# The softmax loop of a hybrid transformer block: one errand in each slot, behind the context products

## What is computed

```python
x = jnp.transpose(query, (1, 0, 2)).reshape(sq * b, h)     # sq = 512, b = 4, h = 256
mixed = (x @ Wqkv.T).reshape(sq, b, nh, 3, hn)             # nh = 16 heads of hn = 16
q, k, v = mixed[..., 0, :], mixed[..., 1, :], mixed[..., 2, :]
# each to (b * nh, sq, hn)
attn = jax.nn.softmax(jnp.einsum('gqd,gkd->gqk', q, k) * norm, axis=-1)
ctx = jnp.einsum('gqk,gkd->gqd', attn, v)
out = ctx.reshape(...) @ Wproj.T + bproj
```

## Time and profile before

| | us |
|---|---|
| time, median of 3 runs | 1167.54 (1164.84 to 1168.75) |
| profiled execution, its own time | 1167.14 |
| its span in the profile | 1165.3 |
| softmax loop, from slot 0 of group 1 to slot 5 of group 7 | 188.6 |
| PE, DVE, ACT busy in the span | 1126.4, 939.7, 774.3 |
| waits of transposed scores (PE's weight loads) for exponentials in the loop | 34.5 |

### The profile page before, as it was taken

The page is one execution under the profiler, slowest core; times in us unless marked ns, Lnnn a source line. Parts: engine busy times, 40 slices in busy tenths (PEclk is TensorE's granted clock), DMA queues, the critical chain, the costliest instruction groups (busy, mean ns, idle before and its releaser), DMA issues. The chain is left out here.

```text
span 1165.3 us, 22548 instructions
## 1 busy us (share of the span) xinstructions
PE 1126.4 (97%) x7599; PEld 908.6 (78%) x7599; DVE 939.7 (81%) x2141; ACT 774.3 (66%) x1535; POOL 629.9 (54%) x1070
## 2 busy tenths in 40 slices
PE   8999999998988999999999999999999999999898
PEld 7444444346766899999999999999999999999876
DVE  6888887866568888888888888888888888888862
ACT  3467676773447767776777777676777677676633
POOL 4020500001715776877786786777687777767520
PEclk9999999999999999999999999999999999999999
DMA  6333333301220102112110201110211211011120
GB/s 186 56 56 57 56 56 57 56 2 38 80 70 23 48 33 84 33 49 69 45 36 33 84 33 49 69 48 33 84 33 43 74 33 48 33 48 33 33 72 1
DMA packets 23450, 60.51 MB, mean 52 GB/s; under 512 B 3367, under 2 KB 8359, under 8 KB 22183
## 3 DMA queue, kind: packets, MB, share of 16 engines
q1 hardware_dynamic: 23335, 59.07, 18.8%
HBM read 44.67 MB, written 2.33 MB: 40 GB/s over the span
## 5 line engine op out<-in xcount | busy, mean ns | idle before, releaser
L1823 DVE SCALAR_TENSOR_TENSOR ln_xn<-l_proj_q,par,ln_xn 128x511 f32<-128x511 f32 (+2 forms) x192 | 142.9, 744 | 97.9 <-ACT ln_xn L1707 95.5
L778 DVE TENSOR_REDUCE a_neg_max<-a_scores 128x1 f32<-128x512 f32 x244 | 155.0, 684 | 30.8 <-PE a_scores L433 28.9
L678 ACT ACTIVATE a_probs<-a_scores_t 128x512 f32<-128x512 f32 x256 | 138.5, 599 | 58.5 <-PE a_scores_t L455 57.3
L96 POOL TENSOR_SCALAR ln_var_eps<-ln_mean_var 128x4 f32<-128x4 f32 (+1 forms) x13 | 3.0, 230 | 283.2 <-DVE ln_mean_var L86 193.3
L1713 ACT ACTIVATE ln_xn<-ln_xn,par 128x512 f32<-128x512 f32 x128 | 92.6, 724 | 94.9 <-DVE ln_xn L1823 94.9
L1412 POOL TENSOR_TENSOR l_k_tok<-l_normed,k_norm 128x384 f32<-128x384 f32 x63 | 64.0, 1016 | 153.9 <-ACT l_normed L1724 153.9
L1823 DVE SCALAR_TENSOR_TENSOR ln_xn<-l_proj_k,par,ln_xn 128x511 f32<-128x511 f32 (+2 forms) x192 | 143.5, 747 | 4.5
L1724 ACT ACTIVATE l_normed<-l_turn_q,l_shift,l_scale 128x128 f32<-128x128 f32 x252 | 95.0, 458 | 21.6 <-POOL l_shift L1405 21.5
L1403 POOL TENSOR_TENSOR l_scale<-l_small,l_minus_half 128x8 f32<-128x8 f32 x64 | 105.1, 1642 | 5.0
L1724 ACT ACTIVATE l_normed<-l_turn_k,l_shift,l_scale 128x128 f32<-128x128 f32 x252 | 95.9, 482 | 0.0
L1781 ACT ACTIVATE l_gate<-l_proj_gv 128x512 f32<-128x512 f32 x64 | 38.2, 597 | 79.0 <-PE l_proj_gv L1491 79.0
(11 more groups left out here) (401 smaller groups left out, 3536.6 us busy)
## 6 DMA issues: line engine op xcount, KB each, us to landing
l_keep<-keep_rows SPq DMA_DIRECT2D x64, 448.0 KB, 3.5
a_stack<-a_dense SPq DMA_DIRECT2D x90, 128.0 KB, 4.3
head_raw<-w_heads SPq DMA_DIRECT2D x8, 1024.0 KB, 6.7
x_tok<-x SPq DMA_DIRECT2D x4, 512.0 KB, 8.2
wo_raw<-w_o SPq DMA_DIRECT2D x1, 2048.0 KB, 10.8
out<-x_tok SPq DMA_DIRECT2D x1, 1920.0 KB
a_stack<-a_max_rows_t SPq DMA_DIRECT2D x64, 4.0 KB
ctx_tok<-w_qkv SPq DMA_DIRECT2D x1, 768.0 KB, 6.7
```

The source lines that it names most:

```text
L678: act.activation(probs[:, n % 2, h, :], scores_t[(4 * n + h) % TURNS][:], ACT.Exp, scale=SOFT_SCALE).then_inc(probs_done, 1)
L778: dve.tensor_reduce(neg_max[:, g % 2, at:at + 1], max_bank(g, j), AX.X, ALU.max, negate=True).then_inc(max_done, 1)
L1823: ins = dve.scalar_tensor_tensor(conv[:, w, m, s:], proj[w][:, 0:SEQ - s], par[:, h, tap:tap + 1], conv[:, w, m, s:], ALU.mult, ALU.add)
```

## The change

Slots of groups 1 to 7 (`gathered(s)`) get one whole errand each, behind the context products, and nothing behind the second scores. The errands are the same; those that stood in two parts are put together: c = 0 turned maxima, c = 1 turned context, c = 2 the first projection with its six matmuls, c = 3 the second, c = 4 and 5 maxima and context again, c = 6 and 7 one bank of values with twelve matmuls or four transposes of tokens. On ACT, the high part of the first projection and the first copy of the values or tokens move from between the two pairs of exponentials to behind them, and stand ahead of `copy_context`. On DVE, the low part in slot 2 moves behind the slot's maxima, and `normalise` from c = 0 and 4 to c = 1 and 5. Group 0 and the slots behind group 7 keep their order.

```diff
+            def whole_errand(s, c):
+
+                projects, values = s + 1 < groups, s + 1 < groups and (s + 1) % KD == 0
+                if c == 0:
+                    if s % KD == 0:
+                        pe.wait_ge(v_copied, copied(s))
+                    elif turned_in(s - 1):
+                        pe.wait_ge(ln.lo_done, KD * (turned_in(s - 1) + 1))
+                    else:
+                        pe.wait_ge(ctx_done, quads * (s - 2) + 1)
+                    transpose_max(s - 1, 1)
+                elif c == 1 and s >= 2:
+                    pe.wait_ge(max_copied, quads * s)
+                    transpose_context(quads * (s - 1) - 1)
+                elif c == 2 and projects:
+                    if s >= 2:
+                        pe.wait_ge(ctx_done, quads * (s - 1))
+                    else:
+                        pe.wait_ge(max_copied, quads * s)
+                    for k in range(KD):
+                        project(s + 1, 0, k)
+                elif c == 3 and projects:
+                    pe.wait_ge(dense_lo_done, 2 * (s + 1) + 1)
+                    for k in range(KD):
+                        project(s + 1, 1, k)
+                elif c == 4:
+                    if projects:
+                        pe.wait_ge(dense_lo_done, 2 * (s + 1) + 2)
+                    else:
+                        pe.wait_ge(ctx_done, quads * (s - 1))
+                    transpose_max(s, 0)
+                elif c == 5:
+                    pe.wait_ge(max_copied, quads * s + 1)
+                    transpose_context(quads * (s - 1))
+                elif c == 6 and values:
+                    pe.wait_ge(ctx_done, quads * (s - 1) + 1)
+                    for e in range(2):
+                        project_values((s + 1) // KD, 0, e)
+                elif c == 7 and values:
+                    pe.wait_ge(v_copied, copied(s + 1) - 1)
+                    for e in range(2):
+                        project_values((s + 1) // KD, 1, e)
...
             def after_context(s, c):
 
                 projects, values = s + 1 < groups, s + 1 < groups and (s + 1) % KD == 0
-                if c == 0 and s >= 1:
+                if gathered(s):
+                    whole_errand(s, c)
+                elif c == 0 and s >= 1:
...
             def after_scores(s, c):
 
                 projects, values = s + 1 < groups, s + 1 < groups and (s + 1) % KD == 0
+                if gathered(s):
+                    return
...
                 if n >= 0:
                     exponentials(n, 1)
+                if gathered(s):
+                    if c == 2 and projects:
+                        split_projection(s + 1, 0)
+                    if c in (6, 7) and turned_in(s):
+                        ln.high(act, turned_in(s), c - 6, misc[:])
+                    if c == 6 and values:
+                        copy_values((s + 1) // KD, 0)
                 if n >= TPB and n % TPB == 0:
                     copy_context(n // TPB - 1)
...
-                if c == 0 and s >= 2:
+                if c == (1 if gathered(s) else 0) and s >= 2:
                     normalise(quads * (s - 1) - 1)
+                if c == 2 and projects and gathered(s):
+                    split_projection(s + 1, 0)
                 if c == 3 and projects:
                     split_projection(s + 1, 1)
-                if c == 4 and s >= 1:
+                if c == (5 if gathered(s) else 4) and s >= 1:
                     normalise(quads * (s - 1))
```

More of the change, by code:

```diff
@@ L258, in copied, with gathered @@
             return 2 * (g // KD) + 2
+        def gathered(s):
+            return 1 <= s < groups
         xt = [[scores_t[1 + k][:] for k in range(KD)]]
@@ L473, in context @@
                 last.then_inc(pv_done, 1)
+            def whole_errand(s, c):
[39 more added lines that the diff above has]
+                        project_values((s + 1) // KD, 1, e)
+                elif c == 6 and turned_in(s):
+                    pe.wait_ge(ctx_done, quads * (s - 1) + 1)
+                    pe.wait_ge(ln.normed, (turned_in(s) + 1) * TPB)
+                    ln.turn(pe, turned_in(s), 0, misc)
+                elif c == 7 and turned_in(s):
+                    pe.wait_ge(ln.lo_done, KD * turned_in(s) + 1)
+                    ln.turn(pe, turned_in(s), 1, misc)
@@ L719, in _ @@
                     copy_max(s - 1, 1)
-                if c == 2 and projects:
+                if c == 2 and projects and not gathered(s):
                     split_projection(s + 1, 0)
@@ L723, in _ @@
                     copy_max(s, 0)
-                if c == 6 and values:
-                    copy_values((s + 1) // KD, 0)
-                if c == 7 and turned_in(s):
+                if c == 7 and turned_in(s) and not gathered(s):
                     ln.high(act, turned_in(s), 1, misc[:])
@@ L735, in _ @@
                     split_projection(s + 1, 1)
-                if c == 5 and turned_in(s):
+                if c == 5 and turned_in(s) and not gathered(s):
                     ln.high(act, turned_in(s), 0, misc[:])
@@ L864, in _ @@
                     add_part(slot - last_max - 2)
[L865 removed]
+                if c == (1 if gathered(s) else 0) and s >= 2:
                     normalise(quads * (s - 1) - 1)
+                if c == 2 and projects and gathered(s):
+                    split_projection(s + 1, 0)
                 if c == 3 and projects:
                     split_projection(s + 1, 1)
[L869 removed]
+                if c == (5 if gathered(s) else 4) and s >= 1:
                     normalise(quads * (s - 1))
[L871 removed]
+                if c == 5 and turned_in(s) and not gathered(s):
                     ln.low(dve, turned_in(s), 0, misc[:])
+                if c in (6, 7) and turned_in(s) and gathered(s):
+                    ln.low(dve, turned_in(s), c - 6, misc[:])
                 if slot == last_max - 3:
```

## The result

The changed kernel takes 1193.68 us (median of 4 runs, 1188.93 to 1195.11) beside 1168.14 us before; the ratio is 1.0211, 95% interval 1.0193 to 1.0229. The profiled execution took 1193.56 us. Its span is 1191.7, 26.4 more than before.

A forecast was written before the change was run, and what follows sets the result against it. The prediction took PE's order of work and its waits for answers, chiefly exponentials, as the bound. Groups 1 to 7 added 3.0 + 3.0 + 3.4 + 3.0 + 3.6 + 2.1 + 1.1 = 19.2 to 1167.1: 1186.5 us, range 1177 to 1194.

The forecast's parts named there:

- The toll in every slot: Every slot of groups 1 to 7 ends in a hand-over of 1.93 us instead of 1.34, 0.6 lost; chance 0.87.
- The step past ACT's copy: After slots 2 and 6, context products wait for ACT's high part (0.47 us) and context copy: hand-over 2.68 us.
- The reason for the toll: At the hand-over, the next transposed score waits for an exponential, as four scores share three banks; 0.6 us missing.
- Two of the signs: In the profile after: PE's waits for exponentials 90 or more in place of 53; all engines' busy times unchanged.
- the clock: Rival, much slower: PE's stops let the clock fall to 1.2 GHz through the loop, over 1240 us; chance 0.03.
- the sum: Rebuilt slots of groups 1 to 7 add 19.2 us, with nothing given back behind the loop: 1186.5 us.
- DVE in lots: Normalising beside token statistics in groups 1 and 3: DVE 0.1 to 0.5 us late; 0.2 added in group 1.
- The range: Whole kernel 1177 to 1194 us, taking in the half-hidden toll's end and DVE late in every slot (1192).
- The half-hidden toll: Rival: in the loop ACT could be ahead of PE after a long errand; half of 19.2 gives 1177; chance 0.04.
- the merged errands as a gain: Rival, faster: in the loop, merges save 3.6 us and slot 2's stall 3, so 1160.5 us; chance 0.04.
- the balance of both: Rival, no change: in the loop tolls and savings cancel, at 0.2 us each instead of 0.6; 1167; chance 0.02.

The follow-up runs named there:

- e2: Changed kernel with the turned context back behind the second scores of slots 0 and 4, and DVE's normalise with it: 1185.28 us, ratio 1.014.
- e3: Changed kernel with whole errands moved behind the second scores, except turned maxima; ACT and DVE copies and splits moved along, context copy first: 1163.59 us, ratio 0.9954.
- e1: Changed kernel with ACT's copy of the context bank ahead of the gathered high parts and value copies: 1185.43 us, ratio 1.0148.
- e4: Changed kernel with exponentials over 256 of the 512 queries in all but the first two chunks: 1180.67 us (two runs).
- e8: From e3, second projection's halves go to slots 2 and 3, second bank of values in two parts to slots 6 and 7: 1156.09 us, ratio 0.9911.
- e5: Changed kernel with each row maximum taken over 256 of the 512 keys: 1188.05 us (two runs, 1184.42 and 1191.68).
- e7: Changed kernel with one more matmul of 512 columns, its result overwritten, ahead of 43 errands in the loop: 1198.96 us, ratio 1.0277.

## Why the prediction came out as it did

**The toll in every slot** held. T to T of the empty slot, 2.95 forecast, measured 2.93; turned maximum 3.16 and 3.35, measured 3.15 and 3.35 (groups 1 and 3 apart, below); projection 4.55, measured 4.53; slot 3 5.28, measured 5.29; group 6 29.6, measured 29.57; group 7 16.4, measured 16.32. e2 and e3 show that the place behind the second scores is what had hidden the work: the same errands there bring the loop below the time of before.

**The step past ACT's copy** held to 0.02 us, and e1 undoes as much of it as DVE's low part allows, 4.2 us of the loop.

**The reason for the toll** was only half right. I read it off the one wait that the timeline named, for the exponential, and off, and set DVE aside because it was busy for only 23 to 25 us of a group. e4 shows that a faster exponential alone gives nothing; DVE's maxima are the last by 0.1 us. The size did not depend on it, since it was taken from a measured boundary. The cure that the prediction names for such a gap, a fourth bank for the transposed scores, was not tried; e4 makes it doubtful that it would help alone. Two of the signs were poor. Busy times were to be unchanged, and PE's grew by 16.7 us. And the count of waits, 90 or more in place of 53, did not come:

```profile
PEld a_scores_t L459 <- ACT a_probs L736: 39.3, 64, 0.8
PE a_scores_t L459 <- ACT a_probs L736: 9.5, 44, 0.2
```

There are 64 such waits of the weight loads in the changed kernel, and in e8, 37 us faster, the same view has 79 with 49.5 us. In group 5 of e8 the loads wait nine times, 5.7 us, while PE has no idle time at all: those waits stood beside running matmuls and cost nothing, and the view of the loads doesn't tell the two apart. The distance between starts does.

**The term that was mis-sized** is the clock. I gave it 0.03 as a rival, and as all or nothing: on through the loop, or off. It fell twice for 3.4 us. Slot 3 of group 4 took 6.85 us instead of the 5.28 of the other groups, slot 7 of group 2 5.51 instead of group 4's 4.28, and the slot behind it 3.68 instead of 3.35: 3.1 us together, of the 4.7 by which the loop exceeded the sum. The two slots of each price show it, in the same kernel, one at 1.2 GHz for half of its time (granted clock 0.75) and one at the full clock:

```profile
157.51:164.37 6.86, 5.94 (x24) 2.68 (x23) 3.17 (x5) 3.04 (x6) 0.00 (x0) 0.75 0.00 0
190.55:195.84 5.29, 4.37 (x24) 2.09 (x24) 3.17 (x5) 3.04 (x6) 0.00 (x0) 1.00 0.00 0
```

Behind the loop, where the kernel is unchanged, 2.7 us more were lost: the clock fell three times in the first 150 us there, once in the kernel before. Counted from the last context product, instruction by instruction, the changed kernel falls behind by 0.8 us at the second of its falls and by 1.3 at the third; the other 0.5 us grow slowly over the rest, and what they come from is open. The same length of both, from shortly before the last context product on, first changed, then before (granted clock 0.97 and 0.99):

```profile
290.54:440.00 149.46, 135.47 (x817) 107.23 (x814) 108.35 (x256) 82.66 (x151) 75.00 (x120) 0.97 0.15 51
```

```profile
266.81:416.27 149.46, 134.79 (x832) 107.17 (x828) 109.92 (x260) 84.92 (x157) 75.24 (x121) 0.99 0.16 53
```

So the sum, which had no term behind the loop, was wrong in this one way. The four executions of the changed kernel say the same: mean clock 0.995 with 1188.93 us, 0.991 with 1193.56 and 1193.81, 0.988 with 1195.11. The execution with the highest mean clock lies 2.4 us from the forecast. The Trainium skill, "TensorE: Matmul & The Clock Gate", section Part 1, says that the default state is the throttled one and that activity releases it; the traces agree in so far as the four kernels whose profile has a fall in the loop (changed, e2, e5, e7) have PE idle for 18.5 to 21.1 us there, and the six without one for 2.7 to 14.5. That is one profile of each, and no run separates the idle time from the moment at which it comes.

**DVE in lots** made most of the rest, 1.6 us: slot 1 of group 3 took 4.11 us instead of 3.53, with the statistics and the maxima close together on DVE. I had seen this risk, charged 0.2 us for it in group 1 and left group 3 to the range. Slots 4 of groups 1 and 3 took 3.51 instead of 3.35, slots 5 3.58 instead of 3.53; with shorter maxima, in e5, both surcharges are gone (3.10 and 3.42, where an empty slot is 2.84). Slots 7 with values took 5.38 instead of 5.28, in e5 too, so that this one is not DVE's (there ACT makes two copies ahead of the context copy, not one).

**The range** held by luck. Its upper end was set by a DVE that is late by 0.1 us in every slot. DVE was late in a few slots only, 1.2 us in all; the clock, which had no term in it, took some 5.3 us (3.1 in the loop, 2.2 behind it) and left 0.3 us to the end.

**The rivals.** The half-hidden toll, the merged errands as a gain and the balance of both fell with the slots of 4.53 and 5.29 us. Merging did save the 0.2 us for each pair (1.60 us for a projection), but inside a slot that had lost its cover. The Trainium skill's rule of matmuls back to back in batches, which the rival of a gain took up, says nothing of the place, and the place decides: the same batches cost 25.5 us ahead of T, and behind the second scores they are part of a kernel 5.5 us faster than before (e3). They are not the gain itself, for e8, which splits half of them again, is faster still.

## What to carry to other kernels

In a loop in which PE hands scores to two engines through a few banks and needs their answers for its next step, look for the boundary where nothing stands between the question and the need; independent work there was free up to the length of the answer (0.6 us here), and behind the context products it cost its full length. Rebuilding each slot from one start to the next, with prices from slots of the same trace, gave every slot of group 5 to within 0.1 us; the misses came where DVE had more to do and where the clock fell. The view of waits named one of the two chains that end together; only shortening each alone and then both showed the other. When a change adds pauses to PE, allow for some falls of the clock, 0.8 to 1.6 us each here, also in the stages behind it.

## What the runs showed of the hardware

A fall to 1.2 GHz lasted 3.4 us wherever a whole one is in the profiles, but for one, and cost 1.5 to 1.6 us in this loop (slot 3 6.85 for 5.29; slots 7 and 0 together 1.6) and 0.8 and 1.3 us in the stages behind it. In e5 one lasted 20.5 us while PE was busy throughout, by its rows. Where it falls is not fixed by the program alone: executions of one kernel differ in their mean clock by up to 0.008 and in time by 5 to 7 us (e1: 0.997 with 1184.96 us, 0.989 with 1190.12; e5: 0.984 with 1191.68, 0.991 with 1184.42). Whether the falls, in the loop and behind it, come from PE's idle time or from a shift in time is open; a run that only shifts the loop was not made.
